# Softmax of eight heads normalised ahead of the transposes, with the values as stationary operand, in the attention of a patch-token, attention and expert kernel

## What is computed

```python
patches = x_padded[:, arange(93)[:, None] * 8 + arange(16)[None, :], :]      # 93 tokens of 16 steps
h = einsum('bnpd,edp->bne', patches, W) + b                                  # (64, 93, 128)

# attention on layernorm(h): projections 128 -> 512 with a causal 3-tap filter per channel
q, k, v = heads(filter3(w1 @ xn)) ; q *= 64 ** -0.5                           # 8 heads of 64
sim = q @ k.T - abs(i - j) * slope[head] ; sim = where(j > i, -big, sim)
h = h + (softmax(sim) @ v).merge_heads() @ wout.T

# experts on layernorm(h): the two best of 16 for each token, silu(x w1) averaged over an expert's tokens
h = h + sum_k routing_w[k] * (mean_over_tokens_of_expert(silu(x @ w1[e].T)) @ w2[e].T)
```

## Time and profile before

| | |
|---|---|
| median of 3 runs | 794.22 us (793.8 to 797.25) |
| profiled execution | 798.25 us, span 796.4 us |
| mean granted TensorE clock | 0.965 |
| TensorE matmuls busy | 742.8 us (93%) |
| TensorE weight loads busy | 691.7 us (87%) |
| VectorE busy | 618.8 us (78%) |
| ScalarE busy | 471.6 us (59%) |
| GpSimd busy | 375.1 us (47%) |

### The profile page before, as it was taken

How to read it: one execution, slowest core, us unless ns; L and a number is a source line. 1 busy time by engine, 2 the same in 40 slices (tenths; PEclk the granted TensorE clock), 3 DMA queues, 4 the chain that set the end, 5 groups by cost and what they waited for, 6 DMA issues and landing times.

```text
span 796.4 us, 20698 instructions
## 1 busy us (share of the span) xinstructions
PE 742.8 (93%) x6770; PEld 691.7 (87%) x6770; DVE 618.8 (78%) x1645; ACT 471.6 (59%) x998; POOL 375.1 (47%) x390
## 2 busy tenths in 40 slices
PE   5678999999999999999999999998998878999986
PEld 4568999999999999999999999997877777999984
DVE  2255878888888888888888888889988648888875
ACT  3444556666566656666655656565543456899960
POOL 3642243666564655655565646554362455122200
PEclk9887999999999999999999999999999968999996
DMA  5421123331221111222111221102124012122205
GB/s 184 140 67 51 40 80 101 127 103 51 57 65 53 49 49 49 53 58 59 49 49 50 68 53 51 50 11 71 33 75 170 19 45 67 51 66 63 62 22 154
DMA packets 44269, 53.97 MB, mean 68 GB/s; under 512 B 13651, under 2 KB 31251, under 8 KB 43696
## 3 DMA queue, kind: packets, MB, share of 16 engines
q1 hardware_dynamic: 30048, 38.84, 16.9%
q0 software_dynamic: 12544, 12.87, 5.8%
q10 hardware_dynamic: 1616, 1.48, 0.6%
HBM read 42.69 MB, written 10.26 MB: 66 GB/s over the span
## 4 chain that ended last, share of the span: by engine, by line
PE 75%; DVE 12%; ACT 4%; issue 3%; DMA 2%; POOL 2%; DVEq 1%; ACTq 0%; SPq 0%
PE psTP L452 10%; PE psSO L590 9%; PE psTP L453 8%; PE psTP L454 8%; PE psSO L672 7%; PE psSO L612 6%; PE psSO L538 4%; PE psTP L524 3%; PE psTP L557 3%; PE psSO L710 3%; PE psTP L710 3%; DMA x_raw<-in_x 2%; PE psTP L635 2%; PE psSO L607 2%; DVE qkv L975 2%
## 5 line engine op out<-in xcount | busy, mean ns | idle before, releaser
L1329 POOL DMA_INDIRECT expert_rows<-hn,slot x128 | 167.6, 1309 | 66.6 <-DVE slot L1177 34.3
L1262 POOL TENSOR_TENSOR x_lo<-x_raw,x_hi 128x752 fp32r<-128x752 f32 x64 | 114.9, 1796 | 142.6 <-ACT x_hi L780 142.6
L975 DVE SCALAR_TENSOR_TENSOR qkv<-psTP,taps,qkv 128x368 f32<-128x368 f32 x192 | 113.9, 593 | 74.6 <-ACT qkv L788 73.2
L788 ACT ACTIVATE qkv<-psTP,taps 128x372 f32<-128x372 f32 x192 | 108.8, 567 | 89.0 <-PE psTP L454 88.7
L978 DVE SCALAR_TENSOR_TENSOR qkv<-psTP,taps,qkv 128x364 f32<-128x364 f32 x192 | 114.6, 597 | 6.8
L452 PE MATMUL psTP<-x_hi,wtok_hi 128*128 128x376 f32 x256 | 94.5, 369 | 13.7 <-DVE wtok_lo L963 9.0
L590 PEld LDWEIGHTS psSO<-vrow,probT 93*93 93x93 f32 x1024 | 94.6, 164 | 4.5 <-ACT probT L830 3.5
L590 PE MATMUL psSO<-vrow,probT 93*93 93x65 f32 x1024 | 95.0, 247 | 1.8 <-DVE resid L1110 0.8
L453 PE MATMUL psTP<-x_lo,wtok_hi 128*128 128x376 f32 x256 | 88.1, 344 | 0.0
L454 PE MATMUL psTP<-x_hi,wtok_lo 128*128 128x376 f32 x256 | 87.8, 343 | 0.0
L452 PE MATMUL psTP<-xnT_hi,wqkv_hi 128*128 128x372 f32 x192 | 77.8, 405 | 9.1 <-DVE qkv L978 5.0
(11 more groups left out here) (193 smaller groups left out, 1577.3 us busy)
## 6 DMA issues: line engine op xcount, KB each, us to landing
x_raw<-in_x SPq DMA_DIRECT2D x64, 376.0 KB, 3.2
w1s<-in_w POOLq DMA_DIRECT2D x8, 512.0 KB, 4.8
w<-in_w SPq DMA_DIRECT2D x4, 1024.0 KB, 6.9
out<-resid SPq DMA_DIRECT2D x16, 160.0 KB, 2.5
xsE<-expert_rows SPq DMA_DIRECT2D x36, 64.0 KB, 2.1
xs<-expert_rows SPq DMA_DIRECT2D x36, 64.0 KB, 1.8
xs<-expert_rows POOLq DMA_DIRECT2D x36, 64.0 KB, 2.1
expert_rows<-hn,slot POOLq DMA_INDIRECT x128, 3.5
```

Of the source, the lines that this page charges most:

```text
L788: nc.scalar.activation(qkv[u][:, k, :, :], psP[(k + 1) % 2][:, 0:GT].rearrange("p (b n) -> p b n", n=NT), ACT.Copy, scale=taps[:, k, 2:3]) ...
L975: nc.vector.scalar_tensor_tensor(dst[:, :, 1:NT], src[:, :, 0:NT - 1], taps[:, k, 1:2], dst[:, :, 1:NT], ALU.mult, ALU.add).then_inc(tap1_ ...
L1262: nc.gpsimd.tensor_tensor(x_lo[u][:, 0:PIECE], x_raw[u][:, :], x_hi[u][:, 0:PIECE].bitcast(F32), ALU.subtract)\
L1329: nc.gpsimd.indirect_dma_start(rows, bass.IndirectOffsetOnAxis(slot[1 - u][:, c:c + 1], 0), hn[1 - u][:, c % GB, :], None)\
```

## The change

- `vrow` loses its column of ones. For each head the values stand (64 columns) and `probT` streams (93 columns). The head with a = 0 writes partitions 0 to 63 of `psO`'s first bank, the one with a = 1 partitions 64 to 127. The output is `attnT` before its copy; `attn` and its four transposes are gone.
- The sums can't come from that product any more, so the softmax is made with tokens on the partitions: VectorE takes the row's extreme value (a minimum, since bias and query scale have changed sign), ScalarE takes exp(minimum - score) for each head apart, eight instructions of 93x93 in two sets of four (`exponentials`), VectorE adds over `prob`, takes the reciprocal and multiplies `prob` by it. Then come the transposes and a plain copy to `probT`. They go to `psPT`, which is `psO`'s first bank and `psV`.
- On each engine `step` has another sequence. TensorE begins a slot with scores and transposes of the probabilities, the second pair of tap products is split up, and the last one stands at the end. ScalarE begins with `high`. On GpSimd the second layer norm's arithmetic stands behind `low`.

The core of the diff:

```diff
-        vrow = [sb(f"vrow{u}", [NT, H, DH + 1]) for u in range(2)]
+        vrow = [sb(f"vrow{u}", [NT, H, DH]) for u in range(2)]
...
+        psPT = [psO[:NT, 0, 0:GT], psV[:NT, 0:GT]]
...
+            def scores(t, u, s, n):
...
+                wait(pe, exp_done, n * 2)
...
+                mm.then_inc(s_mm, 1)
+
+            def turn_prob(t, f, s, n):
+
+                pe.wait_ge(prob_ready, n)
+                wait(pe, res_add, n - 1)
+                pe.wait_ge(v_evac, n)
+                if f.scat and s == 1:
+                    wait(pe, rwT_evac, t - 4)
+                for a in range(2):
+                    for hh in range(4):
+                        mm = nc.tensor.transpose(psPT[a][:, hh * NT:(hh + 1) * NT], prob[:, a, hh, :], ident[:NT, :NT])
+                    mm.then_inc(p_tr, 1)
...
+            def weigh(s, n):
+
+                pe.wait_ge(p_evac, n * 2)
+                pe.wait_ge(v_evac, n)
+                for hh in range(4):
+                    for a in range(2):
+                        mm = nc.tensor.matmul(psO[64 * a:64 * a + 64, 0, hh * NT:(hh + 1) * NT],
+                                              vrow[(s + 1) % 2][:, 2 * hh + a, :], probT[:, a, hh, :],
+                                              start=True, stop=True)
+                mm.then_inc(pv_mm, 1)
...
+            def exponentials(a):
+
+                for hh in range(4):
+                    i = nc.scalar.activation(prob[:, a, hh, :], psS[:NT, a, hh * NT:(hh + 1) * NT], ACT.Exp,
+                                             bias=rmin[:, a, hh:hh + 1], scale=-1.0)
+                i.then_inc(exp_done, 1)
...
+                    if f.attn:
+                        dve.wait_ge(s_mm, n + 1)
+                        nc.vector.tensor_reduce(rmin[:, :, :], heads(psS, NT), AXX, ALU.min).then_inc(min_done, 1)
...
                     if f.proj:
                         conv(t, u, 3 * s)
-                    if prev:
-                        o = heads(psO, DH + 1)
-                        dve.wait_ge(pv_mm, n)
-                        nc.vector.reciprocal(rden[:, :, :], o[:, :, :, DH]).then_inc(den_done, 1)
...
                     if f.attn:
-                        dve.wait_ge(s_mm, n + 1)
-                        nc.vector.tensor_reduce(rmax[:, :, :], heads(psS, NT), AXX, ALU.max).then_inc(max_done, 1)
...
+                        dve.wait_ge(exp_done, n * 2 + 2)
+                        nc.vector.tensor_reduce(den[:, :, :], prob[:, :, :, :], AXX, ALU.add).then_inc(den_done, 1)
+                        dve.wait_ge(den_done, n + 1)
+                        nc.vector.reciprocal(rden[:, :, :], den[:, :, :]).then_inc(rden_done, 1)
                     if f.gate and s == 3:
                         rank(t - 4, u)
+                    if f.attn:
+                        dve.wait_ge(rden_done, n + 1)
+                        nc.vector.tensor_tensor(prob[:, :, :, :], prob[:, :, :, :],
+                                                rden[:, :, :].unsqueeze(3).broadcast_to([NT, 2, 4, NT]),
+                                                ALU.mult).then_inc(prob_ready, 1)
```

More of the change, by code:

```diff
@@ L571, in step @@
                         mm.then_inc(tok_tr, 1)
+                    if f.proj:
+                        proj(t, u, f, 3 * s)
+                    if f.gate and s == 2:
+                        wait(pe, hn_ready, t - 3)
+                        wait(pe, base_done, t - 4)
+                        for b in range(GB):
+                            mm = nc.tensor.transpose(psHn[:, b * NT:(b + 1) * NT], hn[u][:, b, :],
+                                                     ident[:NT, :NT])
+                        mm.then_inc(hnT_tr, 1)
@@ L631, in step @@
-                    if prev:
-                        pe.wait_ge(norm_done, n)
-                        for j in range(QB):
-                            mm = nc.tensor.transpose(psV[:, j * NT:(j + 1) * NT], attn[:, j * 128:(j + 1) * 128],
-                                                     ident[:NT, :NT])
-                        mm.then_inc(a_tr, 1)
-                    if f.gate and s == 2:
-                        wait(pe, hnT_evac, t - 3)
-                        for b in range(GB):
-                            mm = nc.tensor.matmul(psGate[:, b * E:(b + 1) * E], hnT[:, b * NT:(b + 1) * NT],
-                                                  wgate[:, :], start=True, stop=True)
-                        mm.then_inc(gate_mm, 1)
-                        if q is not None:
-                            up_quad(q, 0, 2)
+                        tok_taps(t, s, 1, 1)
@@ L668, in step @@
                         pe.wait_ge(a_evac, n)
-                        if f.gate and s == 3:
-                            wait(pe, base_done, t - 3)
                         for j in range(QB):
@@ L676, in step @@
                         up_quad(q, 0, QUAD)
+                    if f.tok:
+                        tok_taps(t, s, 3, 1)
+                    if f.gate and s == 2:
+                        wait(pe, hnT_evac, t - 3)
+                        for b in range(GB):
+                            mm = nc.tensor.matmul(psGate[:, b * E:(b + 1) * E], hnT[:, b * NT:(b + 1) * NT],
+                                                  wgate[:, :], start=True, stop=True)
+                        mm.then_inc(gate_mm, 1)
+                        if q is not None:
+                            up_quad(q, 0, 2)
+                    if f.scat and s == 0:
+                        wait(pe, rw_done, t - 4)
+                        wait(pe, v_evac, n + 1 if f.attn else B)
+                        nc.tensor.transpose(psRT, rw[:, :, :].rearrange("p b e -> p (b e)"),
+                                            ident[:NT, :NT]).then_inc(rwT_tr, 1)
                     if isinstance(t, int) and t == NG and s == 1:
@@ L825, in step @@
                     q = quad(t, s)
+                    if f.tok and f.more(t, s):
+                        ac.wait_ge(x_in[(s + 1) % 2], t * (16 * GB // 2) + (16 * ((s + 1) // 2) + 16))
+                        high(t * GB + (s + 1), (s + 1) % 2)
                     if prev:
@@ L864, in step @@
-                    if f.gate and s == 1:
-                        wait(ac, scattered[u], (t - u - 4) * (16 * GB))
-                        normalise(t - 4, rstd2, shift2, hn[u], ln2_shift, hn_ready)
+                    if f.proj:
+                        tap2(t, u, 3 * s)
+                    if f.attn:
+                        ac.wait_ge(min_done, n + 1)
+                        wait(ac, p_tr, n * 2)
+                        exponentials(1)
+                    if prev:
+                        ac.wait_ge(pv_mm, n)
+                        wait(ac, out_mm, n - 1)
+                        nc.scalar.activation(attnT[:, :, :].rearrange("p j n -> p (j n)"), psO[:, 0, 0:GT],
+                                             ACT.Copy).then_inc(a_evac, 1)
@@ L900, in step @@
                         nc.scalar.activation(wqkv_hi[:, :, :], wqkv_raw[:, :, :], ACT.Copy).then_inc(wqkv_hi_done, 1)
+                    if f.gate and s == 1:
+                        wait(ac, scattered[u], (t - u - 4) * (16 * GB))
+                        normalise(t - 4, rstd2, shift2, hn[u], ln2_shift, hn_ready)
+                    if f.norm and s == 2:
+                        normalise(t - 1, rstd, shift, xn, ln_shift, xn_ready)
                     if isinstance(t, int) and t == 0 and s == GB - 1:
@@ L1359 @@
     i, j = np.arange(NT)[:, None], np.arange(NT)[None, :]
-    alibi = np.stack([np.where(j <= i, (j - i) * 0.5 ** (h + 1), -1e30) for a in range(2) for h in range(a, H, 2)], 1)
+    alibi = np.stack([np.where(j <= i, (i - j) * 0.5 ** (h + 1), 1e30) for a in range(2) for h in range(a, H, 2)], 1)
     misc = np.zeros((128, C_END), np.float32)
```

260 lines of the change are left out of this document (98 added, 162 removed).

## The result

The changed kernel takes **818.53 us** (median of 4 runs, 817.4 to 819.68), the kernel before 794.35 us (4 runs beside them): a ratio of **1.0291, 95% interval 1.0271 to 1.0312**, so about 3% slower. The profiled execution has a span of 817.2 us against 796.4, which is +20.8. The forecast was 807 us, with a range up to 822: the direction was right, and the size was about twice what was forecast.

The account below looks back on a forecast made before the run. TensorE, busy 50.00 us in 50, was taken as the bound, giving way to rings of waits between engines. Terms of +7, +7.5, -1 and 0 made about +13 on 794.22: 807 us, range 790 to 822.

Parts of the forecast that it names:

- Removed from TensorE: TensorE, each slot: four transposes go (0.36 us), product with the values from 1.30 to 0.90; a group then needs 33.6.
- Exponentials: ScalarE, each slot: eight exponentials of 93x93, 0.34 us each and 0.25 apart, +2.0 us; faster from 0.19 apart down.
- ScalarE's load: ScalarE's busy time in the loop, as a sign of being right: 40 us in 50.
- The rings: Waits between engines in each slot: 8.58 us over VectorE and ScalarE, 8.66 through TensorE; a group 37.2 against 36.6.
- ring 2: The ring through TensorE: from VectorE's sum to the transposes 3.59 us, from there to the next sum 5.07, together 8.66.
- plain slots: Slots s = 1 and s = 2, without VectorE's routing on their path: 8.66 and 9.0 us.
- The wait ahead of the sum: VectorE's sums of `prob` wait for ScalarE each slot, some 1.5 us in plain slots; a sign of being right.
- 12 x 0.6 = +7: Loop t = 4 to 15: twelve groups with taps and gate, each 37.2 us against 36.6, +7 us.
- VectorE and GpSimd block each other: Rival: `x_lo` on GpSimd delays VectorE's multiplication 0.9 us a slot, +50 us, about 857 us; chance 0.05.
- the ring's term for the routing, 1.63: VectorE's routing between convolution k2 of s = 2 and the minimum of s = 3: 8.58 + 1.63 = 10.2 us.
- t = 16 and 17: Two groups without taps: 72.6 us where they take 65.1 in the kernel before, +7.5 us.
- Head, t = 3 and t = 18: Outside the main loop: head 0, give or take 2 us; t = 3 0; t = 18, without projections, -1.

Follow-up runs that it names:

- exp_two: Changed kernel with two exponentials of 93x372, without the row minimum's shift, in place of eight of 93x93: 784.17 us, ratio 0.9843 to the kernel before.
- halves_apart: Changed kernel with the column halves of the product with the values run one after the other instead of alternating: 829.58 us, ratio 1.0418 to the kernel before.
- pool_order: Changed kernel with GpSimd issuing the scatter of slots s = 2 and s = 3 earlier, VectorE's work the same: 800.96 us, ratio 1.0056 to the kernel before.
- k1early: Changed kernel with VectorE's convolution k1 moved ahead of the wait for the exponentials: 793.47 us, ratio 0.9955 to the kernel before.
- all_three: Changed kernel with convolution k1 ahead of the wait, routing behind the minimum of s = 3, and GpSimd's scatter earlier: 766.82 us, ratio 0.9616 to the kernel before.

## Why the prediction was right and wrong

**Removed from TensorE: right.** Rows of the changed kernel, first the product, then what follows it:

```profile
414.68 0.87 PE L576 MATMUL psSO<-probT,vrow 93*64 93x93 f32 x16
415.47 0.44 PE L453 MATMUL psTP<-xnT_hi,wqkv_hi 128*128 128x372 f32 x1
```

0.79 from start to start, 0.049 a pass, in the forecast's 0.04 to 0.055; taken were 0.90. The Trainium skill's rule on weight loads (TensorE: Matmul & The Clock Gate, Part 3, The mechanism), that they overlap a running matmul only when the row groups differ, does not hold here: both halves use the same rows, and the prediction's estimate from the page's load figure was 1.75. (The same section also lets a load run ahead into a background weight buffer; no run here tells whether that is what happens.)

**Exponentials: right within 0.03.** 0.339 each as summed (0.34), 0.22 apart where 0.25 was taken; by the prediction's own sum the change would have paid from 0.19 down. ScalarE's load was put at 40 in 50 us all the same and is 36.17; no sum of the forecast uses it.

**The rings: right.** In the rows the multiplied probabilities take ring 2's path as written: from the sum's start (409.26) to the transposes (412.81) 3.55 where 3.59 was summed, from there to the next sum (417.79) 4.98 where it was 5.07. The plain slots are 8.53 and 8.92 against 8.66 and 9.0; without the waits on GpSimd 9.97 and 9.46 against 10.2 and 9.3. exp_two and halves_apart show that the ring through TensorE rules the plain slots. The wait ahead of the sum is shorter than the 1.5 us forecast, because the statistics (414.61 to 415.99) and in s = 0 `place` stand in it too. By the first minima of the slots, the twelve groups t = 4 to 15 took 106.79 to 546.43 before, 439.6, and now:

```profile
97.20 0.92 DVE L1065 TENSOR_REDUCE rmin<-psSO 93x8 f32<-93x744 f32 x1
...
560.26 0.93 DVE L1065 TENSOR_REDUCE rmin<-psSO 93x8 f32<-93x744 f32 x1
...
630.72 0.92 DVE L1065 TENSOR_REDUCE rmin<-psSO 93x8 f32<-93x744 f32 x1
```

560.26 - 97.20 = 463.1, which is +23.4 where the step "12 x 0.6 = +7" stood. In pool_order the same twelve take 445.1 (97.48 to 542.62), +5.5: the forecast's +7.

**The step that failed** is the rival "VectorE and GpSimd block each other", at 0.05. It looked at the multiplication alone, as the one new instruction with two inputs in SBUF, and put it clear of `x_lo` in time. That much was nearly right (it lasts 0.96 on average, 0.93 when free). But the ring's term for the routing, 1.63, was read in an order where `gap` is free; in the new one it takes 2.25 (431.40 to 433.65), and `place` was put at nothing, as hidden behind the exponentials. An order that shifts in time moves everything that stands in it. `gap` and `wden` are in both kernels, 0.14 and mostly 0.15 us long in the old one, where `x_lo` starts some 3 us behind `gap` and ends 2.7 us ahead of `wden`. Now they last 0.82 and 2.50. `gap` stands ahead of the minimum, on the ring, and its 0.68 is what the distance s2 to s3 has over pool_order's (10.67 against 9.97). `wden` stands behind the minimum of s = 0, where the exponentials cover most of its 2.35; 0.7 is left in s3 to s0 (10.17 against 9.46). With the falls of the clock that is 463.1 - 445.1 = 18 us. The Trainium skill (SBUF — State Buffer, Who interferes with whom) has the rule, that a VectorE instruction with two inputs in SBUF shuts out, and is shut out by, a GpSimd instruction that reads SBUF, one in a two-port mode any GpSimd instruction, until the one that came first has ended. The trace agrees in kind: work of 0.15 us is held to 2.50 and ends with `x_lo`. It differs in one point: `gap` at 417.71 in k1early waits for an `x_lo` that is recorded from 417.81. `wden`, with one input, could fall under the rule by its mode alone; no run here shows its mode. I had cited the rule and applied it to one instruction.

**t = 16 and 17: right in size.** 630.72 - 560.26 = 70.5 against 65.1, +5.4; forecast +7.5.

**Head, t = 3 and t = 18: missed by 7 us**, which hid nearly half of the other miss. +20.8 in all less 23.4 and 5.4 leaves -8.0 for what lies ahead of t = 4 and behind t = 17; forecast 0 and -1. It shows in the fill: the first minimum of t = 3 comes at 62.17, where the first maximum came at 73.05. The table by stretches, before:

```profile
50.00:70.00 20.00, 14.00 (x57) 12.24 (x55) 10.27 (x24) 8.49 (x16) 6.18 (x8) 0.74 0.21 59
```

and after:

```profile
50.00:70.00 20.00, 16.83 (x114) 15.07 (x115) 13.44 (x29) 13.12 (x30) 9.70 (x9) 0.91 0.22 60
```

Before, TensorE stood idle for 3.30 us at 56 to 59 us behind a convolution and then worked at the lower clock; now its longest pause there is 1.68, behind a normalisation, and the clock is 0.91. Which of the moved pieces of ScalarE's and VectorE's sequence does it was not tested.

So 818.5 came out of a loop that cost 16 more than forecast and a head that gave back 8. Without that the time would have been some 826 us, outside the range. That the range held it is luck: the mechanism that it rested on is right, but a cost that it put at nothing and a gain that it did not see partly cancelled.

## What to carry to other kernels

A dependency ring that passes VectorE, ScalarE and TensorE is worth summing; it gave the slots here to 3%. An instruction that waits for another engine wants other work ahead of it on its own engine: one convolution and the routing placed there turned 3% slower into 2.5% faster, with the same instructions. And when an order is changed, look at every small VectorE instruction that works in SBUF alone (here those with two inputs and the addition of a constant were held, reductions were not) and at what GpSimd does beside its new place, not only at the instructions that are new.

## What I had not expected of the hardware

- An instruction of 4 columns can show 2.50 us as its own duration, ending with the GpSimd subtraction beside it (to 0.05 us). A busy time that grew (VectorE 45.05 against 42 to 43) was a wait in disguise; the mean of a group against its shortest instance shows it.
- The hold works the other way as well. An indirect DMA on GpSimd that starts beside a multiplication lasts longer, 1.86 at 387.79 in all_three (the multiplication runs 387.55 to 388.48) where 1.29 is usual. Between 100 and 640 us of all versions 218 of the 258 indirect DMAs that start while a multiplication runs last over 1.5 us, and none of the 955 beside no multiplication does. In pool_order `xnT_lo` takes 1.61 (425.57, beside the multiplication at 425.42), where it takes 0.97 to 1.00 in the kernel before.
- Two column halves of one product, both with float32 and the same rows, overlap when they alternate (0.049 us a pass) and less when they don't (0.073).
- TensorE's clock fell from 2.4 to 1.2 GHz behind an idle time of 1.19 us in a stage where it was 90% busy, but only in every third group, though the idle time was the same in all. With 0.74 to 0.78 in its place it stayed at 2.4. What decides between the groups is open.
